# Beta from ScalarE to GpSimd, and the router's tokens behind the next logits, in a graph convolution with a mixture of experts

## The reference

```python
E = softmax(V_e @ sigmoid(lhs @ rhs + b_e))           # temporal, 16 x 16 per batch
x_tat = einsum('bnfj,bjt->bnft', x, E)
S = softmax(V_s @ sigmoid(lhs2 @ rhs2 + b_s))         # spatial, 256 x 256 per batch
for k in range(3):
    r = einsum('mn,bmn,bmft->bnft', cheb[k], S, x)
    out = out + einsum('bnft,fo->bnot', r, Theta[k])
y = relu(res + conv_over_time(relu(out)))
y = (y - mean_t(y)) / sqrt(var_t(y) + 1e-5) * gamma + beta
x = x + y
```

## Time and profile before

| | |
|---|---|
| median of three executions | 689.44 us (686.73 to 690.37) |
| the profiled execution | 687.6 us |
| its span, first to last instruction | 685.8 us |
| mean granted TensorE clock | 0.889 |
| busy: PE, PEld, DVE, ACT, POOL | 538.0, 363.6, 395.7, 253.8, 198.6 us |
| instructions | 11952 |

### The profile page before, as it was taken

One profiled execution on the slowest core, in us unless ns is written; L12 is line 12 of the kernel. 1 busy time (PEld: TensorE's weight loads), 2 busy tenths in 40 slices (PEclk: granted clock), 3 DMA queues, 4 the chain that ended last, 5 costly groups with the idle time before them and its releaser, 6 DMA issues.

```text
span 685.8 us, 11952 instructions
## 1 busy us (share of the span) xinstructions
PE 538.0 (78%) x2664; PEld 363.6 (53%) x2665; DVE 395.7 (58%) x1697; ACT 253.8 (37%) x619; POOL 198.6 (29%) x267
## 2 busy tenths in 40 slices
PE   0557279989999999999983309999999999999243
PEld 0223147767776677676762204666666666665122
DVE  4745123788888888888899652333333333332265
ACT  0435833443444444444432201333333333333232
POOL 5000000113333333333334430434433433434000
PEclk9989558999999999999996557999999999999555
DMA  9900000000000000000010141222222222221697
GB/s 304 423 7 2 0 1 0 1 1 25 32 34 30 32 32 32 32 34 30 32 39 32 39 132 55 85 78 88 84 83 87 84 84 90 84 84 35 206 298 231
DMA packets 36260, 52.86 MB, mean 77 GB/s; under 512 B 4605, under 2 KB 31360, under 8 KB 35968
## 3 DMA queue, kind: packets, MB, share of 16 engines
q1 hardware_dynamic: 24816, 30.86, 14.3%
q0 software_dynamic: 6480, 16.85, 6.6%
q10 hardware_dynamic: 4928, 4.72, 2.1%
HBM read 30.19 MB, written 23.14 MB: 78 GB/s over the span
## 4 chain that ended last, share of the span: by engine, by line
PE 47%; DVE 31%; DMA 8%; issue 7%; ACT 4%; SPq 1%; POOL 1%; DVEq 0%; POOLq 0%; ACTq 0%
PE bank L614 18%; PE bank L629 9%; DMA xT<-yrows 5%; DVE vq L1012 4%; PE bank L492 4%; PE bank L601 2%; PE bank L622 2%; DVE vq L1011 2%; PE bank L377 2%; DVE work L1173 2%; PE bank L459 2%; DVE work L1189 2%; ACT xs L714 2%; DVE work L1224 1%; PE bank L367 1%
## 5 line engine op out<-in xcount | busy, mean ns | idle before, releaser
L614 PE MATMUL bank<-w,xT 128*128 x284 | 137.5, 607 | 2.0 <-DVE xT L1413 2.0
L1413 DVE COPY xT<-bank 128x256 f32<-128x256 f32 x71 | 30.2, 425 | 145.8 <-PE bank L601 145.8
L978 POOL DMA_INDIRECT yrows<-xT,dest x71 | 69.6, 980 | 141.1 <-ACT xT L834 137.0
L492 PE MATMUL bank<-work 128*128 128x256 f32 x384 | 95.0, 391 | 0.0
L946 POOL DMA_INDIRECT xrows<-xtok,slot x64 | 67.2, 1050 | 92.2 <-DVEq L1310 75.1
L492 PEld LDWEIGHTS bank<-work 128*128 128x128 f32 x384 | 71.9, 194 | 9.6 <-issue 0.8
L629 PE MATMUL bank<-w,xT 128*128 x284 | 73.3, 380 | 1.6 <-ACT xT L839 1.6
L935 POOL TENSOR_TENSOR yg<-work,sml 128x512 f32<-128x512 f32 x16 | 17.9, 1121 | 191.2 <-DVE work L1224 191.2
L614 PEld LDWEIGHTS bank<-w,xT 128*128 128x128 f32 x284 | 49.4, 194 | 38.1 <-issue 38.1
L828 ACT ACTIVATE xT<-bank 128x256 f32<-128x256 f32 x71 | 27.3, 384 | 97.4 <-PE bank L614 97.4
L629 PEld LDWEIGHTS bank<-w,xT 128*128 128x128 f32 x284 | 48.5, 190 | 6.2 <-issue 2.6
(11 more groups left out here) (200 smaller groups left out, 993.2 us busy)
## 6 DMA issues: line engine op xcount, KB each, us to landing
xT<-xrows SPq DMA_DIRECT2D x71, 129.0 KB
xT<-yrows SPq DMA_DIRECT2D x32, 256.0 KB, 3.9
xs<-x_in SPq DMA_DIRECT2D x4, 1024.0 KB, 10.2
w<-w13t_in SPq DMA_DIRECT2D x1, 4096.0 KB, 18.4
out<-xT ACTq DMA_DIRECT2D x16, 256.0 KB, 4.1
w<-w2t_in SPq DMA_DIRECT2D x1, 2048.0 KB, 22.8
yrows<-xT,dest POOLq DMA_INDIRECT x71, 2.4
xrows<-xtok,slot POOLq DMA_INDIRECT x64
```

The costliest lines, as they stand in the source:

```text
L492: last = mm(bank[6][:, h * N:(h + 1) * N], z[:, p, c, k, h], A[:, p, c, k], start=(c == 0 and k == 0), stop=(c == C - 1 and k == K - 1))
L614: last = mm(bank[2 + q][:, :], xc[:, q, c], w13[:, e, c].rearrange("p w n -> p (w n)"), start=(c == 0), stop=(c == C - 1))
L978: pool.indirect_dma_start(yrows, bass.IndirectOffsetOnAxis(ap=dest[:, q], axis=0), yo[:, q], None, bounds_check=2 * TOKENS - 1, oob_is_err ...
L1413: V.tensor_copy(xc[:, q].rearrange("p c k -> p (c k)"), bank[q][:, 0:C * P]).then_inc(c_xc, 1)
```

## The change

Beta is no longer added in stage 1; GpSimd adds it in `ln_out` of each turn, between the product with gamma and the addition to x. `tokens` and `turn_logits` go from the end of a TensorE turn into the next turn, for the same batch: `tokens` behind `logits`, `turn_logits` behind the first six graph matmuls. ScalarE does `copy_tokens` at the head of the next turn, and `normalise` goes to the end of the turn, behind `tanh` and the second `copy_features`. On VectorE `route_a` leaves the statistics and becomes the head of the chain of `route_b`.

```diff
@@ TensorE
             def turn(i, q, ahead2, ahead1, now, back1, back2, back3):
                 if ahead1:
                     logits(i + 1, 1 - q)
+                if back3:
+                    tokens(i - 3, 1 - q)
                 if now:
                     graph(i, q, 0, 0)
+                if back3:
+                    turn_logits(i - 3, 1 - q)
+                if now:
                     graph(i, q, 0, 1)
...
                 if back3:
                     prefix(i - 3, 1 - q)
-                if back2:
-                    tokens(i - 2, q)
-                if back2:
-                    turn_logits(i - 2, q)
@@ ScalarE
-            def add_beta(first, end):
-
-                act.wait_ge(a_xnv, B)
-                act.wait_ge(a_xna, B)
-                for t in range(first, end):
-                    nc.scalar.activation(x_all[:, :, :, t], x_all[:, :, :, t], ACT.Identity,
-                                         bias=sm("beta")[:, t:t + 1], scale=1.0).then_inc(x_beta, 1)
...
             normalise_and_copy(1, 6, GB + 2)
-            add_beta(0, T // 2)
             temporal_tanh(1)
-            add_beta(T // 2, 3 * T // 4)
             temporal_exp(1)
-            add_beta(3 * T // 4, T)
...
             def turn(i, q, ahead2, ahead1, now, back1, back2, back3):
+                if back3:
+                    copy_tokens(i - 3, 1 - q)
                 if back1:
                     square(i - 1, 1 - q)
...
                 if ahead1:
                     copy_features(i + 1, 1 - q, 0)
-                if back2:
-                    normalise(i - 2, q)
                 if ahead2:
                     tanh(i + 2, q)
                 if ahead1:
                     copy_features(i + 1, 1 - q, 1)
                 if back2:
-                    copy_tokens(i - 2, q)
+                    normalise(i - 2, q)
@@ GpSimd
             def ln_out(b, p):
                 pool.wait_ge(s["b_dn"], done(b))
-                step = Steps(pool, p_x1, b, 1)
+                step = Steps(pool, p_x1, b, 2)
...
                 step(nc.gpsimd.tensor_tensor(flat(yg[:]), flat(y[:, p]), over(sm("gamma")), ALU.mult))
+                step(nc.gpsimd.tensor_tensor(flat(yg[:]), flat(yg[:]), over(sm("beta")), ALU.add))
...
-            pool.wait_ge(x_beta, T)
@@ VectorE
-                choice = router(route_b)
+                def choose():
+                    yield from router(route_a)
+                    yield from router(route_b)
+
+                choice = choose()
                 weave(centre())
-                weave(router(route_a), statistics())
+                weave(statistics())
```

More of the change, by code:

```diff
@@ L245, in build @@
         v_ln = sem("v_ln"); v_gn = sem("v_gn"); v_rt = sem("v_rt"); v_rt2 = sem("v_rt2"); v_rt3 = sem("v_rt3"); v_lq = sem("v_lq"); v_gq = sem("v_gq")
-        p_x1 = sem("p_x1"); x_beta = sem("x_beta"); v_mx = sem("v_mx")
+        p_x1 = sem("p_x1"); v_mx = sem("v_mx")
         sc_done = [sem("sc_done0"), sem("sc_done1")]
@@ L705, in normalise_and_copy @@
                         copy_x(g, j - 2)
-            x_all = xs[:].rearrange("p b c (o t) -> p (b c) o t", t=T)
-            def add_beta(first, end):
-                act.wait_ge(a_xnv, B)
-                act.wait_ge(a_xna, B)
-                for t in range(first, end):
-                    nc.scalar.activation(x_all[:, :, :, t], x_all[:, :, :, t], ACT.Identity,
-                                         bias=sm("beta")[:, t:t + 1], scale=1.0).then_inc(x_beta, 1)
             normalise_and_copy(0, 0, GB + 2)
```

## The result

The kernel after takes **677.7 us** (median of four executions, 675.9 to 679.8) against 688.5 for the kernel before in the same comparison: ratio **0.9846, 95% interval 0.9819 to 0.9872**, 10.8 us faster. Two more comparisons gave 0.9845 and 0.9844. The forecast was 682.0 (677.5 to 687.5). The profiled execution took 677.07 us, with a span of 675.2 and a granted clock of 0.903.

A forecast was written before the change was run, and what follows sets the result against it. VectorE's instruction list was taken to bound the turns, ScalarE's queue the end of stage 1. Terms -7.2 - 1.1 + 1.3 + 1.8 - 1.4 = -6.6 us gave 681.0 to 682.8, forecast 682.0 us, range 677.5 to 687.5.

The forecast's parts named there:

- Stage 1, -7.2: End of stage 1: without ScalarE's beta additions, tanh and exponential directly follow VectorE, so the sum comes 7.2 us earlier.
- The first turns, -1.1: Turn 2 to 3: TensorE's and ScalarE's order brings the variance 1.4 us earlier, less 0.27 for GpSimd's addition: 1.1 us gained.
- The steady turns, +1.3: Turns 4 to 14: each pays 0.27 us for GpSimd's addition and gains 0.15 from VectorE's order, 1.3 us slower over 11.
- The price of the addition, +0.27: Each turn: GpSimd's third instruction holds a small VectorE operation, which then ends 0.27 us later.
- The -0.15 for VectorE's order: Each turn: route_a leaving the statistics saves 0.30 us, its operations cost 0.15 in the router's rounds, net -0.15 us.
- rearrangement gives nothing: After the first turns TensorE is ahead of VectorE; its idle 1.5 us return as a later wait for pn, gain 0.
- Turns 15 and 16, +1.8: Turns without big products there: GpSimd's third instruction holds another small VectorE operation, 0.9 us each, 1.8 us slower.
- Turn 17, -1.4: Turn 17: the last batch's statistics go ahead of route_a, which waits for the transposed gate; everything to the last scatter 1.4 us earlier.
- VectorE kept its gap of 0.03 us: Rival, turns 2 to 14: VectorE's small operation comes second behind the beta addition; turns grow 1.25 us, about 694 us; chance 0.07.
- A turn paid 0.10 and not 0.44: Rival: addition costs 0.44 and moved router operations 0.3, so turns grow 0.44 us; 685.5 us, or 687.5 with low clock; chance 0.15.
- TensorE alone was not the bound: Rival: TensorE bounds the turns and the change removes its stall, 17 us over 12 turns, giving 665 us; chance 0.03.
- Stage 1 gave its all: Rival, stage 1: something other than ScalarE holds the temporal part, so nothing is gained there; 689 us; chance 0.04.

The follow-up runs named there:

- the third comparison: The changed kernel once more, unaltered, against the kernel before, beside the kernel with beta added early in three pieces: 676.63 us, ratio 0.9844.

## Why the prediction was right, and where it wasn't

The direction, the range and the terms held; that the number fell inside the range is partly luck. 677.7 lies 0.2 us above its lower end, and the third comparison's 676.6 would have been below it. The five priced stretches give -6.6 us in the first profile, the very sum of the forecast, but only because a fall of the clock in turn 15 took 1.5 us back; in the third, without that fall, they give -8.3. Some 4 us of the gain lie outside the sum.

**Stage 1, -7.2.** Measured -7.3 from A to M, in every kernel without the additions. Two pairs of kernels that differ by nothing else show that the time passes on to the end: 7.75 us, and 10 ± 3 us by the ratios 0.9845 and 0.9991. The profiles give 7.3 + 2.7 - 2.2 = 7.8: the 2.7, an average over few profiles, are the clock between M and G1, where I had kept "the same course as now, and ±2", and it is the largest term that the sum lacked. Against it stand the 2.2 us by which A came later in the kernels without the additions, unexplained.

**The first turns, -1.1.** Measured -1.4 to -1.5 (G2 to G3 15.59 for 17.05, the addition's share in it), with the mean's matmul 6.75 us behind the logits' start where the step had 5.46 + 1.3. The step, however, gave the gain to TensorE's order, "1.4 at the variance". That order alone gives 0.6, because the router's copy in front of the statistics then waits 1.73 us for the transpose. VectorE's order takes the copy out of the way, and only with both is it 1.75 (17.32 to 15.57).

**The steady turns, +1.3.** Measured +0.8: 11 x (0.28 - 0.18) = 1.1 by the separate kernels, and G3 to G14 gives 0.65 to 0.8, as not all eleven turns are alike (17.05 to 17.5 in the kernel before). The price of the addition, +0.27, was met to a hundredth in the old orders (17.32) and in the new (17.15 - 16.87 = 0.28), by the operation that the step named. The -0.15 for VectorE's order came out as -0.18, but the step behind it, that from turn 4 on TensorE's "rearrangement gives nothing", has failed. It gives nothing alone, and VectorE's order alone costs 0.13, since the variance's matmul becomes the next limit. The two parts of VectorE's price were right: the row maximum comes 0.3 earlier, and the moved operations take 0.13 back. I had looked for what is late next behind TensorE's change and not behind VectorE's.

**Turns 15 and 16, +1.8.** The addition costs 0.83 behind G15 and 0.81 behind G16, 1.64 in all, by one operation more that is held in each, as priced. The new orders give back 0.66 between G14 and G16, which the sum hadn't. G14 to G15 takes 15.8, 16.2 and 17.3 us in three profiles of the kernel after; in the one with 17.3 six graph matmuls take 2.3 us instead of 1.5, and the clock is at 0.5 for 3.4 us. That alone makes the difference between the first profile and the third.

**Turn 17, -1.4.** The orders give -1.58 from G16 to S, of which VectorE's has all (14.56 for 16.12).

**What the sum had not** are the clock ahead of G1, and turns in which TensorE's clock falls. A steady turn with such a fall costs 1.7 us. Six were seen in four profiles with TensorE's old order, none in nine with the new one. In the kernel before that is one in two profiles, some 0.8 us on average. With beta on GpSimd and the old order it is two or three such turns. That accounts for the small gain of beta moved alone, 0.5 to 1 us, where its parts give 2.9: -7.3 from A to M, -2.7 from M to G1, +2.2 ahead of A, +4.9 in the turns and the drain.

The rivals fall. VectorE kept its gap of 0.03 us. A turn paid 0.10 and not 0.44 (by that rival's own terms it would be 0.41: 0.27 and the 0.14 by which 1.27 exceeds 1.13). TensorE alone was not the bound: its order alone gave a steady turn nothing (17.33 for 17.32). Stage 1 gave its all.

## What to carry to other kernels

Work given to an idle engine isn't free if it holds up operations of the one that bounds, as GpSimd's additions did to VectorE's small operations here: look for stretches in which the bounding engine runs only operations that aren't touched, and put it there, in pieces that end before the next one that is. The same additions cost 7 to 10 us on ScalarE's queue in front of a chain of short steps, 6 us beside the turns, 6 us as one row early, and nothing that could be measured in three pieces. And when two queues are reordered, each order alone is no measure of the two together: find for each what would be late next.

## What the runs showed of the hardware

- A small VectorE operation was held for a whole **row** of GpSimd instructions, 6.25 us, and not until the end of the one that was running. The row had no gaps: its instructions, 1.12 us long, start 1.09 us apart. In the turns, where GpSimd's instructions wait for each other by a semaphore, they start 1.20 us apart, and VectorE gets in between them: its operation at 217.76 starts in the gap ahead of the one at 217.79, and the one at 218.72 ends at 218.93, before the third instruction starts at 219.00. The Trainium skill (SBUF — State Buffer, "Who interferes with whom") says that whoever issues first has the shared pair for the whole instruction; by that rule the hold would have been over with the instruction that was running, at 89.0, after 0.8 us. The measurement decides. That the missing semaphores make the difference was not tried by itself.
- Not only operations with two inputs in SBUF are held: among those above are a TENSOR_SCALAR (6.25 us) and a COPY (L1238, 1.12 us) with one. The Trainium skill, in the same section (SBUF — State Buffer, "Who interferes with whom"), exempts instructions with one SBUF input only outside the modes that use both ports, and says that copies and tensor_scalar can enter these; the trace agrees. Beside GpSimd's additions these were not held: the one reduction of a PSUM bank (0.69 us, in the row above) and the products with an operand in PSUM (0.94 to 0.96).
- TensorE's clock fell in single turns of a steady loop (0.91 over such a turn, +1.68 us), in which TensorE does the same work in the same order as in its neighbours. It did so in six steady turns of four profiles with the old order of TensorE's queue and in none of nine with the new one. Four profiles are few, and why the order would matter isn't shown.
